# Lambda of all batches ahead of the pipeline, with a 0/1 product for the heads, and result-free products ahead of waits

## The reference, cut to what matters

```
k = softmax((x @ Wk + bk) as [b, 1, 16, t], over t)
v = bn((x @ Wv + bv))     as [b, 1, 16, t]
lam_c = einsum('bukt,buvt->bkv', k, v)          # 16 x 16 for each batch
Yc    = einsum('bhkt,bkv->bhvt', q, lam_c)      # the same lambda for all 8 heads
lam_p = relu(conv3x3(v, Wpos));  Yp = einsum('bhkt,bkvt->bhvt', q, lam_p)
Y = Yc + Yp;  h = h + Y @ Wout + bout
```

## Time and profile before

| what | us |
|---|---|
| median of three runs | 630.47 |
| lowest, highest run | 624.87, 630.87 |
| the profiled execution | 626.53 |
| its span, first to last instruction | 624.7 |
| mean granted TensorE clock | 0.975 |
| TensorE busy | 583.1 (93%) |
| VectorE busy | 461.2 (74%) |
| ScalarE busy | 259.5 (42%) |
| GpSimd busy | 252.6 (40%) |

### The profile page before, as it was taken

How to read it: one execution, slowest core, us unless ns; L and a number is a source line. 1 busy time by engine, 2 the same in 40 slices (tenths; PEclk the granted TensorE clock), 3 DMA queues, 4 the chain that set the end, 5 groups by cost and what they waited for, 6 DMA issues and landing times. The chain is left out here.

```text
span 624.7 us, 13320 instructions
## 1 busy us (share of the span) xinstructions
PE 583.1 (93%) x3737; PEld 466.9 (75%) x3737; DVE 461.2 (74%) x1313; ACT 259.5 (42%) x652; POOL 252.6 (40%) x266
## 2 busy tenths in 40 slices
PE   2599999999999999999898999999999899999993
PEld 0467888888888888888665777777777788888882
DVE  6979889999999987887685677877788654444441
ACT  3432333333333333232133465656565555555551
POOL 2923325555445553221132235454545343333332
PEclk9899999999999999999996899999999999999997
DMA  8402455666555555544566635454442232222210
GB/s 276 59 1 88 149 176 183 198 205 197 182 175 175 180 171 172 166 142 152 162 123 176 175 91 147 123 130 110 110 109 62 77 90 82 66 69 68 71 32 2
DMA packets 127171, 80.02 MB, mean 128 GB/s; under 512 B 66548, under 2 KB 121485, under 8 KB 127126
## 3 DMA queue, kind: packets, MB, share of 16 engines
q1 hardware_dynamic: 121586, 72.63, 41.1%
q0 software_dynamic: 3296, 6.27, 3.1%
q10 hardware_dynamic: 2244, 0.55, 0.5%
HBM read 30.64 MB, written 49.33 MB: 128 GB/s over the span
## 5 line engine op out<-in xcount | busy, mean ns | idle before, releaser
L1230 DVE SCALAR_TENSOR_TENSOR P<-PS,QN 128x512 f32<-128x512 f32 x128 | 79.5, 682 | 28.6 <-PE PS L1405 28.6
L551 DVE SCALAR_TENSOR_TENSOR Z<-PS,Vt,Z 126x128 f32<-126x128 f32 x224 | 78.6, 351 | 8.7 <-PE PS L679 0.6
L679 PE MATMUL PS<-Wh,Ah 128*126 128x512 f32 x256 | 78.4, 429 | 0.0
L679 PE MATMUL PS<-Wl,Ah 128*126 128x512 f32 x256 | 70.8, 398 | 3.4 <-DVE Wl L515 3.4
L339 POOL TENSOR_TENSOR INCl<-INC,INCh 126x512 fp32r<-126x512 f32 x31 | 40.1, 1292 | 77.0 <-ACT INCh L415 77.0
L679 PE MATMUL PS<-Wh,Al 128*126 128x512 f32 x256 | 70.3, 396 | 0.0
L791 POOL DMA_INDIRECT out_h<-LC,KVH x39 | 37.9, 971 | 69.7 <-DVE LC L830 67.0
L679 PEld LDWEIGHTS PS<-Wl,Ah 128*126 128x126 f32 x256 | 48.3, 189 | 16.1 <-issue 3.8
L848 PE MATMUL PS<-W1h,IM 128*128 x156 | 58.8, 417 | 0.1
L679 PEld LDWEIGHTS PS<-Wh,Al 128*126 128x126 f32 x256 | 47.7, 186 | 12.3
L455 ACT ACTIVATE XT<-PS 128x126 f32<-128x126 f32 x32 | 8.8, 276 | 107.9 <-PE PS L727 107.9
(11 more groups left out here) (219 smaller groups left out, 1340.5 us busy)
## 6 DMA issues: line engine op xcount, KB each, us to landing
routed<-nobody SPq DMA_DIRECT2D x30, 1170.0 KB, 5.2
IM<-v_pad SPq DMA_DIRECT2D x124, 72.0 KB
KVH<-routed SPq DMA_DIRECT2D x39, 130.0 KB, 2.1
WRW<-in_w SPq DMA_DIRECT2D x16, 256.0 KB, 3.0
R<-h_rows SPq DMA_DIRECT2D x16, 129.9 KB
W1l<-in_wsig SPq DMA_DIRECT2D x4, 512.0 KB, 9.6
W<-in_w SPq DMA_DIRECT2D x8, 256.0 KB, 4.0
q_raw<-QS SPq DMA_DIRECT2D x32, 63.0 KB
```

The source lines that it names most:

```text
L551: ins = dve.scalar_tensor_tensor(Z[:, u], psU[h][:, d], sc, Z[:, u], ALU.mult, ALU.add)
L679: ins = pe.matmul(out, a, w, start=(n == 0), stop=(n == len(turn) - 1))
L1230: ins = dve.scalar_tensor_tensor(P[:, b, HV * h:HV * h + HV], psC[2 * pair + hb], 0.0, QN[:, g % 2, b:b + 1].broadcast_to([128, HV, SP]), ...
```

## The change

The lambda of all 64 batches is computed without the eightfold copy of the keys: lam(n) multiplies the 16 key columns of a pair by its 32 value columns and leaves 16 x 32 in psM. ScalarE copies that to LAM (lam_out), and one product with a 0/1 matrix (spread, 16 rows to 128 columns, from the constants K_CI, which grow by 112 columns) puts it on the partitions of all heads; ScalarE copies the result to LS, which now holds all groups. This goes in three portions, LAMBDA = (0, 2, 9, 16): groups 0 and 1, groups 2 to 8, groups 9 to 15. lam(0) and spread(0) stand ahead of step 0, lam(1), spread(1) and lam(2) in step 0, spread(2) in step 1. The block at L1506 and the copies at L1133 and L1160 go from all steps. GpSimd takes LC of a group from its part of LS, and its VC half of groups 8 to 15 moves behind LC and QN of step 0. The output product waits for lg_ready of the step before (for all of LS in step 1). In step 0 and step 1 result-free products are added, 2 or 3 at a time, and their target bank is 4 instead of 5. SP's routed rows wait for the third spread instead of the last lambda block.

```diff
-K_END = K_CI + 2 * DK - 1
+K_END = K_CI + DK - 1 + 128
...
-            sp.wait_ge(lam_done, NG)
+            sp.wait_ge(spread_done, 3)
...
-        KH = KVH[:, 3 * NB * DK // 2:2 * NB * DK].rearrange("p (u b h k) -> p u b h k", u=2, b=GB // 2, h=NH)
+        LAM = KVH[0:DK, 3 * NB * DK // 2:5 * NB * DK // 2]
...
-        LS = sb("LS", [128, GB * DK])
+        LS = sb("LS", [128, NB * DK])
...
-        psL = PS[7][:, 0:GB * DK].rearrange("p (b v) -> p b v", b=GB)
+        LAMBDA = (0, 2, 9, NG)
+        psM, psL = (PS[7][0:DK, 0:128], PS[5][0:DK, :], PS[5][0:DK, :]), (PS[7][:, 128:256], PS[7][:, :], PS[7][:, :])
...
@@ GpSimd @@
-                if k == 0:
-                    pool.wait_ge(v_ready, 5)
-                    gs = slice(4, G8)
-                    pool.tensor_tensor(VC[:, gs, 3:6], three_shifts(gs), VC[:, gs, 0:3].bitcast(f32), ALU.subtract).then_inc(v_ready, 1)
                 if on(k, 0, NG):
-                    pool.wait_ge(ls_ready, k + 1)
+                    pool.wait_ge(ls_ready, sum(k >= g for g in LAMBDA[:3]))
...
+                if k == 0:
+                    pool.wait_ge(v_ready, 5)
+                    gs = slice(4, G8)
+                    pool.tensor_tensor(VC[:, gs, 3:6], three_shifts(gs), VC[:, gs, 0:3].bitcast(f32), ALU.subtract).then_inc(v_ready, 1)
...
@@ ScalarE @@
+            def lam_out(n):
+
+                lo, hi = GB * DK * LAMBDA[n], GB * DK * LAMBDA[n + 1]
+                act.wait_ge(lam_done, n + 1)
+                act.activation(LAM[:, lo:hi], psM[n][:, 0:hi - lo], ACT.Copy).then_inc(lam_ready, 1)
+                act.wait_ge(spread_done, n + 1)
+                act.activation(LS[:, lo:hi], psL[n][:, 0:hi - lo], ACT.Copy).then_inc(ls_ready, 1)
...
-                if on(k + 1, 0, NG):
-                    wait_from_one(act, lam_done, k)
-                    act.activation(KH[:, w], KT[:, (k + 1) * GB // 2:(k + 2) * GB // 2].unsqueeze(2).broadcast_to([128, GB // 2, NH, DK]),
-                                   ACT.Copy).then_inc(kh_ready, 1)
+                if k == -1:
+                    lam_out(0)
                 if k == -1:
                     act.wait_ge(v_ready, 4)
                     gs = slice(4, G8)
                     act.activation(VC[:, gs, 0:3], three_shifts(gs), ACT.Copy).then_inc(v_ready, 1)
+                    lam_out(1)
+                    lam_out(2)
...
-                if on(k + 1, 0, NG):
-                    act.wait_ge(lam_done, k + 2)
-                    wait_from_one(act, lc_ready, k + 1)
-                    act.activation(LS[:], psL.rearrange("p b v -> p (b v)"), ACT.Copy).then_inc(ls_ready, 1)
...
@@ TensorE @@
+            def lam(n):
+
+                if n == 2:
+                    pe.wait_ge(lam_ready, 2)
+                p = range(GB // 2 * LAMBDA[n], GB // 2 * LAMBDA[n + 1])
+                for b in p:
+                    c = 2 * DK * (b - p.start)
+                    ins = pe.matmul(psM[n][:, c:c + 2 * DK], KT[:, b], VT[:, b].rearrange("p h j r -> p (h j r)"), start=True, stop=True)
+                ins.then_inc(lam_done, 1)
+
+            def spread(n):
+
+                lo, hi = GB * DK * LAMBDA[n], GB * DK * LAMBDA[n + 1]
+                pe.wait_ge(lam_ready, n + 1)
+                if n:
+                    pe.wait_ge(ls_ready, n)
+                pe.matmul(psL[n][:, 0:hi - lo], K[0:DK, K_CI + DK - 1:K_CI + DK - 1 + 128], LAM[:, lo:hi], start=True, stop=True).then_inc(spread_done, 1)
...
             def step(k):
                 w, f, g = (k + 1) % 2, k - 2, k - 1
+                if k == 1:
+                    keep_busy(pe, 3, PS[4][:, :], S1h[:])
+                    spread(2)
+                    keep_busy(pe, 3, PS[4][:, :], S1h[:])
                 if on(k, 1, NG):
                     conv(k, 1)
...
                 if on(k, 0, NG):
                     conv(k, 2)
+                if g == 0:
+                    keep_busy(pe, 2, PS[4][:, :], S1h[:])
...
-                    pe.wait_ge(ls_ready, min(k + 1, NG))
+                    if g == 0:
+                        pe.wait_ge(ls_ready, 3)
+                    else:
+                        pe.wait_ge(lg_ready, g)
...
                 if k == 0:
-                    keep_busy(pe, 2, PS[5][:, :], S1h[:])
+                    lam(1)
                 if on(k, 0, NG):
                     conv(k, 3)
...
+                if g == 0:
+                    keep_busy(pe, 3, PS[4][:, :], S1h[:])
...
                 if k == 0:
-                    keep_busy(pe, 2, PS[5][:, :], S1h[:])
+                    keep_busy(pe, 2, PS[4][:, :], S1h[:])
                 if on(k, 0, NG):
                     add_products(k, 0)
+                if g == 0:
+                    keep_busy(pe, 2, PS[4][:, :], S1h[:])
...
-                if on(k + 1, 0, NG):
-
-                    pe.wait_ge(kh_ready, k + 2)
-                    if on(g, 0, NG):
-                        pe.wait_ge(lg_ready, g + 1)
-                    for b in range(GB // 2):
-                        ins = pe.matmul(psL[:, 2 * b:2 * b + 2], KH[:, w, b].rearrange("p h k -> p (h k)"),
-                                        VT[:, (k + 1) * GB // 2 + b].rearrange("p h j r -> p (h j r)"), start=True, stop=True)
-                    ins.then_inc(lam_done, 1)
+                if k == 0:
+                    keep_busy(pe, 2, PS[4][:, :], S1h[:])
+                    spread(1)
+                    lam(2)
                 if on(k + 1, 1, NG):
                     conv(k + 1, 0)
             keep_busy(pe, 6, PS[0][:, :], S1h[:])
             conv(0, 0)
             pe.wait_ge(kvt_ready, 3)
-            step(-1)
-            keep_busy(pe, 3, PS[5][:, :], S1h[:])
+            lam(0)
+            keep_busy(pe, 3, PS[4][:, :], S1h[:])
+            spread(0)
             conv(0, 1)
```

More of the change, by code:

```diff
@@ L751, in experts @@
     routed, out_rows = m["routed"], m["out_rows"]
-    scattered, lam_done, table_ready, lg_ready, bs_ready, pos_ready, w2_in = shared
+    scattered, spread_done, table_ready, lg_ready, bs_ready, pos_ready, w2_in = shared
     IC = I // 128
@@ L941, in middle @@
         conv_done, p_ready, qn_ready, lc_ready, sum_done = sem("conv_done"), sem("p_ready"), sem("qn_ready"), sem("lc_ready"), sem("sum_done")
-        kh_ready, lam_done, ls_ready, yc_done, yc_ready = sem("kh_ready"), sem("lam_done"), sem("ls_ready"), sem("yc_done"), sem("yc_ready")
+        lam_done, lam_ready, spread_done, ls_ready, yc_done, yc_ready = sem("lam_done"), sem("lam_ready"), sem("spread_done"), sem("ls_ready"), sem("yc_done"), sem("yc_ready")
         ht_done, h1_ready, mv_ready, sd_ready, xn_ready = sem("ht_done"), sem("h1_ready"), sem("mv2_ready"), sem("sd2_ready"), sem("xn2_ready")
@@ L985, in middle @@
         on_sp, on_pool, on_act, on_dve, on_pe = experts(
-            m, ctx, sem, KVH, P, IM, LC, (scattered, lam_done, table_ready, lg_ready, bs_ready, pos_ready, w2_in))
+            m, ctx, sem, KVH, P, IM, LC, (scattered, spread_done, table_ready, lg_ready, bs_ready, pos_ready, w2_in))
         block = ctx.enter_context(nc.Block())
@@ L1069, in step @@
                 w, f, g = (k + 1) % 2, k - 2, k - 1
-                if k == 0:
-                    pool.wait_ge(v_ready, 5)
-                    gs = slice(4, G8)
-                    pool.tensor_tensor(VC[:, gs, 3:6], three_shifts(gs), VC[:, gs, 0:3].bitcast(f32), ALU.subtract).then_inc(v_ready, 1)
                 if on(k, 0, NG):
-                    pool.wait_ge(ls_ready, k + 1)
+                    pool.wait_ge(ls_ready, sum(k >= g for g in LAMBDA[:3]))
                     wait_from_one(pool, yc_done, k - 1)
-                    pool.tensor_tensor(LC[:, k % 2], LS[:].unsqueeze(2).broadcast_to([128, GB * DK, NH]),
+                    pool.tensor_tensor(LC[:, k % 2], LS[:, GB * DK * k:GB * DK * k + GB * DK].unsqueeze(2).broadcast_to([128, GB * DK, NH]),
                                        K[:, K_MB:K_MB + NH].unsqueeze(1).broadcast_to([128, GB * DK, NH]), ALU.mult).then_inc(lc_ready, 1)
@@ L1579, in lay_out @@
     K[0:DK, K_RV:K_RV + DK] = np.eye(DK)[::-1]
-    K[:, K_CI:K_END] = (np.arange(2 * DK - 1)[None, :] + 1 - np.arange(128)[:, None]) % DK == 0
+    K[:, K_CI:K_END] = (np.arange(DK - 1 + 128)[None, :] + 1 - np.arange(128)[:, None]) % DK == 0
     K[np.arange(128), K_BD + 24 + np.arange(128) // DK] = 1
```

## The result

| | before | changed |
|---|---|---|
| median, us | 627.80 (4 runs, 624.87 to 630.87) | 641.31 (4 runs, 639.42 to 644.36) |
| the profiled execution | 626.53 | 640.76 |
| its span | 624.7 | 639.0 |
| mean granted clock | 0.975 | 0.970 |

The account below looks back on a forecast made before the run. TensorE's issue order was taken to bound the pipeline, waits and a fallen clock the start-up. 5.85 us (steps) plus 0.35 (start-up) made 6.2 us less, 620.3 by profile, 624.3 by median; forecast 622 us, range 616 to 629.5.

Parts of the forecast that it names:

- Steady steps: Steps 2 to 14: leaving the block out of TensorE's order saves 13 x 0.45 = 5.85 us; moving LC costs nothing.
- Rival 2: Steps 2 to 14: VectorE or the YC-h1-xn chain swallows the saving, TensorE waits at L1405; 626 to 630 us, chance 0.12.
- steady term: The block's removal from the 13 steps 2 to 14, at 0.45 us each: 5.85 us saved.
- Products in front: Lambda products moved ahead of the steady steps: 0.034 us a record, lam(1) and lam(2) 0.95 us each, a spread 1.0 with wait.
- Rival 3: Start-up: narrow lambda products pay their weight loads in series, 0.088 us a record, +3.0 us, 623.3 us; chance 0.10.
- Start-up: First convolution to step 2: +3.2 us to step 1's second convolution, -3.55 us behind it at full clock; 0.35 us gained.
- ledger: Item-by-item account of the start-up from the first convolution to step 2, which would start at 346.9 instead of 347.26.
- rival 1: Start-up: the clock falls despite the fillers, step 2 starts 7.6 us later; 628.3 us, or 632.2 on the median's basis; chance 0.15.
- The basis of the sum: Savings set on the profiled execution give 620.3 us, on the median 624.3; the middle, 622 us, was taken.

Follow-up runs that it names:

- e1: Changed kernel, with GpSimd's LC made to wait until up of the step before is done, its old place; 623.46 us, ratio 0.9923.
- e2: Kernel before, plus one extra GpSimd operation of LC's form with constant operands ahead of LC from step 5 on; 649.24 us, ratio 1.0312.
- e10: Changed kernel with a one-column GpSimd memset between the scatter and LC, timed in 12 runs; 622.80 us, ratio 0.9917.
- e11: Kernel before with an extra LC-shaped GpSimd operation, and a one-column memset between the scatter and it; 624.17 us in one run.
- e8: Changed kernel with LC held back, plus two result-free 128 x 32 fp32 products at the block's place in steps 2 to 14; 626.23 us, ratio 1.0023.
- e7: Kernel before plus 15 result-free products in step 1 (8 ahead of conv(1,1), then 2, 3 and 2), nothing else; 622.35 us, ratio 0.9946.
- e6: Changed kernel with LC held back, without the 15 result-free products that the change added; 622.88 us, ratio 0.9960.
- e9: Changed kernel with LC held back, five result-free products fewer (three behind spread(2), two ahead of spread(1)); 620.64 us, ratio 0.9867.
- e3: Changed kernel plus eight result-free products ahead of conv(k,2) in odd steps from 5 on; 636.73 us, ratio 1.0156.
- e5: Changed kernel with a one-column GpSimd memset between the scatter and LC; 621.64 us in one run.
- e4: Changed kernel with an empty GpSimd instruction ahead of LC; 644.36 us, ratio 1.0275.

## Why the prediction was wrong

**The step that failed** is in "Steady steps": "GpSimd's LC no longer waits for LS and moves up; nobody waits for it." It is true of the semaphores and was costed at nothing. But LC moved from behind VectorE's choice to right behind the scatter, and there LC and the two QN lengthen three operations of the choice by 2.4 us. The excess over e1's steps is 3.5 to 3.6 us in steps 5, 7, 9, 11 and 14 and 2.0 in step 13, 19.8 us of the 20.0 between the two kernels. It is shown by e1 (taken away: gone), by e2 (added to the kernel before: there) and by e10 and e11 (LC kept early, separated from the scatter by 0.11 us of work: the long steps are gone). The Trainium skill has this contention in SBUF — State Buffer, section "Who interferes with whom": a VectorE instruction with two SBUF inputs contends with a GpSimd instruction that reads SBUF, casts and tensor_scalars may too, reduces never do, and the block lasts for the whole instruction. The traces agree: eq 0.19 to 1.86 us, the cast 0.16 to 1.81, reduces 0.19, P unchanged. The prediction moved a GpSimd instruction without asking what VectorE does beside it at its new place.

**Rival 2** was right in the place (the wait for P at conv(k,2)) and wrong in cause and size: it let VectorE swallow a saving of 0.45 us, up to 630, and had no way to lose more than that. The saving isn't swallowed, for it stands in the steps 3, 4, 6, 8, 10 and 12.

**The block**: 0.45 us from start to start was 0.37 in the step, so the steady term is 4.8 instead of 5.85 us. e8 shows it, and the traces show where the other 0.08 us is. Before, the block starts 0.12 us behind the start of the last product of the shared expert and the convolution 0.45 us behind the block, 0.57 us together. Without the block, in e1, the convolution starts 0.22 us behind that product, not 0.12, so only 0.35 us comes back by these starts. The last product before the change, then the same one and the convolution in e1:

```profile
377.34 0.28 PE L1426 MATMUL PS<-X2l,S1h 128*128 128x252 f32 x1
```
```profile
376.71 0.28 PE L1450 MATMUL PS<-X2l,S1h 128*128 128x252 f32 x1
376.93 0.73 PE L1411 MATMUL PS<-IM,W 36*128 36x512 f32 x4
```

The distance between two starts was an upper estimate of what leaving the block out gives back.

**Products in front**: right. 28 records of lam pass in 0.92 us (0.95 forecast), a spread of 448 columns in 0.94 with its wait (1.0 forecast). Rival 3 falls: 0.033 us a record, while the loads record 0.097 us each (28 of them would be 2.7 us in series), though all these loads use all rows. The changed kernel's start-up:

```profile
330.56 1.01 PE L1430 MATMUL PS<-KVH,K 16*128 16x448 f32 x2
331.51 0.99 PE L1421 MATMUL PS<-KVH 128*16 128x32 f32 x28
332.43 0.51 PE L1410 MATMUL PS<-IM,W 36*128 36x512 f32 x2
...
335.58 0.50 PE L1410 MATMUL PS<-IM,W 36*128 36x512 f32 x2
...
344.96 0.73 PE L1410 MATMUL PS<-IM,W 36*128 36x512 f32 x4
```

**Start-up**: from the first convolution to conv(1,1) 13.19 us against 13.13 by the ledger. That agreement is partly luck: the first convolution of step 1 came 0.34 us earlier than forecast (10.04 us behind the start instead of 10.38), and each group of three result-free products behind it took 0.89 us instead of 0.65, since 0.213 us for one was too little. From there to step 2 9.38 against 10.2, 22.57 in all where 23.3 was forecast, at a clock of 1.00. The gain was 1.1 us instead of 0.35; rival 1 didn't occur in this execution. What the ledger missed is what it is made of: e7 has the result-free products alone and needs 20.11 us, so the keeping of the clock gives 3.6 us and the moved lambda takes 2.5 of them back. Set side by side by profiles, the lambda's move is worth 4.8 - 2.5 = 2.3 us, and the result-free products 3.6. By medians it is 2.6 us for the move alone (e6) and 3.1 for the products alone (e7), with overlapping intervals, so which is the larger isn't shown. That the clock of this stretch depends on the products alone isn't shown either: in e6 and e9 it was low before the places that differ, and it was 1.00 in e1 and e8. The profiles differ most in how long it stayed low once it had fallen: some 3.5 us in e3 and e5, which have all 15 products, 10 us in e9, which has ten of them, and 24 us in e6, which has none of the 15. These are single profiles, and the falls came at different moments, so it is a trend and no proof.

**The basis of the sum.** The prediction took the median from three runs, 630.47 us, 3.9 us above the profiled execution. A fourth run (625.12) brings it to 627.80, 1.3 us above. The forecast would move by some 0.4 us, little beside the 20 us that were lost in the steps.

**The rest of the span**, +1.5 us: the choice of step 14 is held as well, and conv(15,2) at 496.72 waits 1.46 us for P where 0.25 us is usual; that is 1.2 of it.

**What stays open.** Why LC directly behind the scatter holds VectorE 0.7 us before LC's own record starts. That LC claims the shared access to SBUF while it stands ready behind the scatter, and that the memset does not (it reads nothing), would fit e1, e5 and e11. It is argued, not shown.

## What to carry to other kernels

When a wait is taken away or an instruction moves up on GpSimd, list what VectorE runs beside it at the new place; semaphores don't show this dependence, but a column of durations does: one operation at 0.19 in one step and 1.86 in the next is held, not slow. A delay on VectorE of 2 us cost TensorE 2 us here and mostly a further 1.5, when its clock fell, so an interference of small operations can outweigh a saving on the bounding engine (here 20.0 us against 4.8). And test result-free products without the reorganisation that they came with: here either alone gave about as much as the other (e7 0.9946; e6, with LC late, 0.9960).

## What the runs showed of the hardware that was not expected

- A GpSimd tensor operation standing directly behind an indirect DMA held VectorE from within the DMA's record: eq began at 373.53, LC at 374.25, and eq ended with LC. The Trainium skill (SBUF — State Buffer, "Who interferes with whom") says that issue order decides who blocks; by the records VectorE was first and still lost, so the start of a GpSimd record doesn't tell the order that counts. One column of memset between the two (0.11 us) removed this early hold, an empty instruction didn't. It doesn't protect an operation that meets a running LC: met, 0.16 us in e1, took 1.08 us in e10.
- Thirteen waits of 2.2 us without products in them stand in the steps 5 to 14 of three profiles (changed kernel, e4, e3's step 14). The granted clock fell behind nine and stayed at 1.00 behind four, among them step 13 (12.15 us) of the changed kernel; e4's steps 5, 7, 9 and 11 take 14.95, 12.05, 13.70 and 13.68 us with the same wait. Behind seven shorter ones in e2, 1.6 to 1.8 us, it fell six times. So the price of such a fall is a range in these traces: 0 to 3 us on top of the wait.
